# Late softmax division, scores in three split products, and experts with stationary weights

## The reference, cut to what matters

```
# layer 1: q from the rows, k and v from context and rows (120 + 256 = 376 keys)
sim = einsum('bhid,bhjd->bhij', q * 64**-0.5, k)
attn = softmax(sim, axis=-1)
out = einsum('bhij,bhjd->bhid', attn, v)
x = x + tanh(g_xattn[0]) * layernorm(out @ w_out)
...
# layer 4: g, u and the hidden layer of four experts, weighted by cw
g = einsum('th,ehi->tei', x, Wg); u = einsum('th,ehi->tei', x, Wu)
mlp_out = einsum('tei,eih->teh', silu(g) * u, Wd)
routed = einsum('te,teh->th', cw[:, :4], mlp_out)
# plus x times other columns of cw, plus a causal convolution of 4 taps
```

## Time and profile before

| | |
|---|---|
| runs (three) | 2227.55 us median, 2222.08 to 2231.18 |
| profiled execution | span 2225.1 us, mean granted TensorE clock 0.994 |
| busy over the span | PE 2186.7 us (98%), DVE 1728.1 (78%), ACT 1282.0 (58%), POOL 645.1 (29%) |
| first stage | about 0 to 1113 us, then the experts to about 1600 us |
| last stage | about 1600 us to the end |

### The profile page before, as it was taken

How to read it: one execution, slowest core, us unless ns; L and a number is a source line. 1 busy time by engine, 2 the same in 40 slices (tenths; PEclk the granted TensorE clock), 3 DMA queues, 4 the chain that set the end, 5 groups by cost and what they waited for, 6 DMA issues and landing times. The chain is left out here.

```text
span 2225.1 us, 48355 instructions
## 1 busy us (share of the span) xinstructions
PE 2186.7 (98%) x15486; PEld 1865.5 (84%) x15486; DVE 1728.1 (78%) x6112; ACT 1282.0 (58%) x3251; POOL 645.1 (29%) x1162
## 2 busy tenths in 40 slices
PE   8999999999999999999999999999999999999997
PEld 6777777777777777777699999999878888888886
DVE  6788888888888888888675555555579999999986
ACT  6776776776776776776443333433345555555553
POOL 1123223222232232232220000000355555555541
PEclk9999999999999999999899999999999999999999
DMA  5320110110110110110052222221212222222210
GB/s 189 124 97 22 37 40 23 37 39 21 40 38 20 39 39 20 40 32 27 11 161 73 81 86 72 81 77 41 89 58 65 65 65 64 65 65 65 65 39 20
DMA packets 111642, 129.57 MB, mean 58 GB/s; under 512 B 14898, under 2 KB 98089, under 8 KB 111264
## 3 DMA queue, kind: packets, MB, share of 16 engines
q1 hardware_dynamic: 98249, 105.06, 14.9%
q0 software_dynamic: 12288, 21.21, 3.3%
q10 hardware_dynamic: 855, 0.19, 0.0%
HBM read 84.26 MB, written 54.53 MB: 62 GB/s over the span
## 5 line engine op out<-in xcount | busy, mean ns | idle before, releaser
L711 ACT ACTIVATE a_prob<-a_prob,a_nmax 128x376 f32<-128x376 f32 x512 | 309.7, 606 | 155.3 <-DVE a_nmax L857 155.3
L1457 ACT ACTIVATE e_hidden<-e_first,keep_b 128x256 f32<-128x256 f32 x320 | 134.1, 471 | 283.3 <-PE e_first L80 282.8
L857 DVE CUSTOM_DVE_ANT_0 a_prob<-a_score,a_mask_row 128x376 f32<-128x376 f32 x512 | 266.6, 540 | 10.8 <-issue 5.6
L80 PE MATMUL e_second<-e_w,e_hidden 128*128 128x256 f32 x1920 | 239.5, 284 | 0.0
L80 PEld LDWEIGHTS e_second<-e_w,e_hidden 128*128 128x128 f32 x1920 | 232.6, 192 | 0.0
L869 DVE TENSOR_SCALAR a_prob<-a_prob,a_rden 128x376 f32<-128x376 f32 x512 | 220.9, 453 | 2.5
L1151 PE MATMUL a_turned<-keep_ident,a_prob 128*128 128x128 f32 (+1 forms) x1536 | 217.3, 277 | 2.8 <-DVE a_probT L876 1.6
L1151 PEld LDWEIGHTS a_turned<-keep_ident,a_prob 128*128 128x128 f32 (+1 forms) x1536 | 173.5, 142 | 43.5 <-issue 27.6
L1142 PE MATMUL a_score<-a_kT,a_qT 64*128 64x376 f32 x1024 | 196.4, 502 | 0.0
L876 DVE COPY a_probT<-a_turned 128x384 f32<-128x384 f32 x256 | 139.8, 546 | 54.4 <-PE a_turned L1151 54.4
L719 ACT ACTIVATE a_probT<-a_turned 128x384 f32<-128x384 f32 x256 | 124.9, 488 | 92.1 <-PE a_turned L1151 91.7
(11 more groups left out here) (237 smaller groups left out, 5231.1 us busy)
## 6 DMA issues: line engine op xcount, KB each, us to landing
w_in<-W SPq DMA_DIRECT2D x32, 512.0 KB, 4.1
slots<-a_zeros SPq DMA_DIRECT2D x8, 1280.0 KB, 8.7
keep_rows<-slots SPq DMA_DIRECT2D x40, 256.0 KB, 3.9
answers<-e_y SPq DMA_DIRECT2D x40, 256.0 KB, 2.2
a_xn<-x SPq DMA_DIRECT2D x32, 256.0 KB, 2.9
a_xr<-x SPq DMA_DIRECT2D x32, 256.0 KB, 3.8
x<-r_x SPq DMA_DIRECT2D x32, 256.0 KB, 4.0
w_in<-x SPq DMA_DIRECT2D x32, 256.0 KB, 2.6
```

Of the source, the lines that this page charges most:

```text
L80: last = nc.tensor.matmul(out, stationary(a, t), moving(b, t), start=start and n == 0, stop=stop and n == len(todo) - 1)
L711: nc.scalar.activation(prob[:, u % 4, a], prob[:, u % 4, a], ACT.Exp, bias=nmax[:, u % 4, a:a + 1], scale=-1.0, accum_out=den[:, u % 4, a: ...
L857: nc.vector.tensor_tensor_reduce(prob[:, u % 4, a], score[SCORE_AT[u][a]][:, 0:NKV], mask_row[:, p], -1.0, 3.0e38, ALU.add, ALU.min, nmax[ ...
L1457: nc.scalar.activation(hidden[:, 2 * j + i], first[:, j, i * CH:(i + 1) * CH], ACT.Relu, bias=b1[:, 2 * j + i, bass.ds(e, 1)]).then_inc(re ...
```

## The change

**First stage.** Scores are a split product: q and k get a low part (`q_low`, `k_low` on DVE), and `scores` issues the three passes, the two heads in turn. The division moves behind `times_v`: `normalise` goes, `turn_prob` takes the bare exponentials, and `attended` on DVE multiplies the result (128x256 per pair of heads) by the reciprocal sums. There these lie along the free axis and are equal on 64 partitions. To get them there, `over_sum` (now once per pair of heads) takes the reciprocal and transposes it in 32x32 blocks, and `spread_shares` on SP writes it to DRAM in four transfers, waits, and reads it back in two that copy it to 64 partitions each. A bank that `q_high` or `k_high` reads is free only after `q_low` or `k_low`. `place`, `choose` and `counts_in` change their places, the router's count moves on PE, and POOL sends a batch's rows in one piece.

**Last stage.** In `gate_up` the weights become stationary and the 256 rows stream: half of the experts (`j`) at a time, 12 matmuls of 256 columns where there were 6 of 512. The hidden layer is then born transposed, `turn_hid` goes, and the router's weight must lie along the free axis: `weights_turned` (DVE), `spread_weights` (SP: four writes, a wait, one read to 128 partitions, 512 KB) bring it there. `share_ups` and `hidden` (DVE, 128x512 each, twice a step) take the place of `weigh`. `silu(1)`, `hidden_low(0)`, `down`, `x3_own` and others change places; `x4p` gets a second buffer.

```diff
+            def spread_shares(b, m):
+                done = KI * b + m
+                eng.wait_ge(rden_ok, done + 1)
+                for g in range(0, P, 32):
+                    eng.dma_start(t["shares"][m, :, g:g + 32], rden_rows[g:g + 2 * QT, m % 2]).then_inc(share_out, 16)
+                eng.wait_ge(share_out, 64 * (done + 1))
+                at_least(eng, att_ok, done - KI + 1)
+                for a in range(2):
+                    eng.dma_start(share[64 * a:64 * a + 64, m], ...).then_inc(share_in[m], 16)
...
+            def k_low(b, m):
+                eng.wait_ge(k_hi, KI * b + m + 1)
+                nc.vector.tensor_tensor(kT[:, 1, m], (bank_b if m < 2 else bank_a)[:, 0:NKV], kT[:, 0, m].bitcast(F32),
+                                        ALU.subtract).then_inc(k_lo, 1)
+            def q_low(b, i):
+                eng.wait_ge(q_hi, 2 * b + 2 - i)
+                nc.vector.scalar_tensor_tensor(qT[:, 1, 2 * i:2 * i + 2], bank_a[:].rearrange("p (m s) -> p m s", m=2),
...
-            def normalise(b, u, a):
-                nc.vector.tensor_scalar(prob[:, u % 4, a], prob[:, u % 4, a], rden[:, u % 4, a:a + 1], None, ALU.mult) \
...
+            def attended(b, m):
+                eng.wait_ge(pv_made, KI * b + m + 1)
+                eng.wait_ge(share_in[m], 32 * (b + 1))
+                nc.vector.tensor_tensor(att[:, m], (bank_a if m == 1 else bank_b)[:, 0:S], share[:, m],
+                                        ALU.mult).then_inc(att_ok, 1)
...
-                    nc.tensor.matmul(score[SCORE_AT[u][a]][:, 0:NKV], qT[rows, p, m, i * P:(i + 1) * P],
-                                     kT[rows, p, m], start=True, stop=True).then_inc(score_ok[a], 1)
+                for n, (high, low) in enumerate(PASSES):
+                    for a in range(2):
+                        rows = slice(64 * a, 64 * a + 64)
+                        last = nc.tensor.matmul(score[SCORE_AT[u][a]][:, 0:NKV], qT[rows, high, m, i * P:(i + 1) * P],
+                                                kT[rows, low, m], start=n == 0, stop=n == len(PASSES) - 1)
...
+            def spread_weights(b):
+                eng.wait_ge(cw_turned, b + 1)
+                for g in range(0, P, 32):
+                    eng.dma_start(t["chosen"][:, g:g + 32], cw_rows[g:g + EM * QT]).then_inc(cw_out, 16)
+                eng.wait_ge(cw_out, 16 * 4 * (b + 1))
+                at_least(eng, share_ok[1], b)
+                eng.dma_start(cw_wide[:].rearrange("p e s -> p (e s)"),
+                              t["chosen"].rearrange("c q -> (c q)").partition_broadcast(P)).then_inc(cw_in, 16)
...
-                for e in range(EM):
-                    es = slice(e * P, (e + 1) * P)
-                    nc.vector.scalar_tensor_tensor(hid[:, i, es], hs[:, i, es], cw[:, p, i, e:e + 1], ups[i][:, es],
+            def share_ups(b, j):
+                eng.wait_ge(cw_in, 16 * (b + 1))
+                nc.vector.tensor_tensor(hid[:, j].rearrange("p (e s) -> p e s", e=2),
+                                        ups[j][:].rearrange("p (e s) -> p e s", e=2), cw_wide[:, pair(j)],
+            def hidden(b, j):
+                nc.vector.tensor_tensor(hid[:, j], hs[:, j], hid[:, j], ALU.mult).then_inc(hid_ok[j], 1)
...
-                split_product(nc, out[i][:].rearrange("p (e i) -> p e i", e=EM),
-                              lambda a, k: x4T[:, a, k, i * P:(i + 1) * P],
+                for e in range(2):
+                    last = split_product(nc, out[j][:, e * S:(e + 1) * S], lambda a, k: weight2(name, a, k)[:, 2 * j + e],
+                                         lambda a, k: x4T[:, a, k], KD)
```

More of the change, by code:

```diff
@@ L928, in step @@
                     weights_lower(3, wo[:], stage_o)
-                if live(s - 2):
-                    normalise(s - 2, 2, 0)
                 if live(s - 3):
-                    att_low(s - 3, 3)
+                    attended(s - 3, 3)
                 if live(s - 2):
@@ L979, in step @@
                     row_max(s - 2, p, 6, 0)
+                if here(s - 4):
+                    choose(eng, s - 4, 4)
+                if live(s - 2):
                     row_max(s - 2, p, 6, 1)
-                    over_sum(s - 2, 4)
-                    normalise(s - 2, 4, 0)
-                    normalise(s - 2, 4, 1)
+                    over_sum(s - 2, 2)
+                if here(s - 4):
+                    choose(eng, s - 4, 5)
+                if live(s - 2):
+                    turned_out(s - 2, 3, 1)
+                    attended(s - 2, 0)
+                if here(s - 4):
+                    choose(eng, s - 4, 6)
+                if live(s - 2):
+                    row_max(s - 2, p, 7, 0)
+                if here(s - 4):
+                    choose(eng, s - 4, 7)
+                if live(s - 2):
+                    row_max(s - 2, p, 7, 1)
+                if live(s - 1):
+                    q_low(s - 1, 1)
+                if live(s - 2):
                     att_low(s - 2, 0)
-                    turned_out(s - 2, 3, 1)
-                    row_max(s - 2, p, 7, 0)
-                    row_max(s - 2, p, 7, 1)
+                if live(s - 1):
+                    k_low(s - 1, 0)
                 if here(s - 3):
@@ L2337, in step @@
                 if live(s - 4):
-                    weigh(s - 4, p, 1)
+                    hidden(s - 4, 0)
+                    relu(s - 4, p)
+                    share_ups(s - 4, 1)
+                    hidden(s - 4, 1)
                 if live(s - 3):
                     silu(s - 3, 0)
+                if live(s - 4):
+                    hidden_low(s - 4, 0)
+                if live(s - 3):
                     route_and_combine(s - 3, q, s, p)
@@ L2366, in down @@
                         eng.wait_ge(wd_low, 1)
[L2367 to L2368 removed]
+                for i in range(QT):
+                    for n, (a, c, e) in enumerate((a, c, 2 * j + e) for e in range(2) for a, c in PASSES):
+                        last = nc.tensor.matmul(total[:, i * D:(i + 1) * D], hid2[:, a, e, i * P:(i + 1) * P],
+                                                wd2[:, c, e], start=j == 0 and i == 0 and n == 0, stop=False,
+                                                skip_group_check=True)
+                last.then_inc(down_made[j], 1)
             def values(b):
```

425 lines of the change are left out of this document (215 added, 210 removed).

## The result

The changed kernel takes 2332.26 us (median of 4 runs, 2329.41 to 2334.39), the one before 2228.14 in the runs beside it: 1.047 times as long, with an interval of 1.0447 to 1.0493. I had forecast slower, but 2276 and at most 2320. The profiled execution has a span of 2329.3 us, 104.2 more than before.

The account below looks back on a forecast made before the run. The prediction took a ring through several engines to bound each changed stage. To 2225.1 us it added 31 (first stage), 13 (last stage) and 6 (ends), 2275.1, and said 2276, with a range of 2190 to 2320.

Parts of the forecast that it names:

- rings: First and last stage: closed paths through several engines, adding up to the step, 33.58 and 18.48 us.
- The chain keeps its length: Last stage, router's chain on DVE up to cws: stays at 5.42 us.
- The middle leg: Last stage, normalise4 to the chain's first operation, 9.14 us: grows by 0.69.
- the first leg: Last stage: cws to normalise4, -0.28 us. Where the choice is discussed: first stage, out_stat to row_max, +1.24.
- the right ring: First stage, path from out_stat through DVE, ACT and TensorE back to out_stat: +1.0 us a step, bounds 0.2 to 1.8.
- By legs: First stage: out_stat to row_max +1.24 us, row_max to router_in's end -0.37, turn_prob to output +0.62.
- the choice: First stage, DVE between out_stat and row_max: about ten tiny operations of choose come in, 0.89 us.
- TensorE's work: TensorE alone would allow steps of 32.9 us in the first stage, 17.4 to 17.8 in the last.
- The round trips: Transfers to DRAM and back, division about 7 us, weights 7.8: covered in the steady state, costed at nothing.
- That the rings might be looser: First rival, both stages: TensorE sets both steps, 2189 us, range 2175 to 2216; chance 0.20.
- The fourth rival: First stage scores: two heads don't overlap in the fast format, blocks of 2.2 us, +90, 2334 in all; chance 0.07.
- the third rival: Last stage: the weights' round trip comes late, 1.4 us a step, +43, 2320 in all; chance 0.12.

Follow-up runs that it names:

- The first experiment: Changed kernel with the last stage's POOL addition (x3p + x4r) cut to two columns per partition: 2301.79 us.
- experiments 4 and 5: Changed kernel without q_low and k_low; the former with three score products of high parts, 2273.83 us, the latter with one full-float32 product, 2289.09 us.
- experiment 4: Changed kernel without q_low and k_low, the scores' three products reading the high parts: 2273.83 us.
- experiment 2: Changed kernel without both round trips through DRAM and the waits for them, reciprocal sums and router's weights constant: 2329.42 us.

## Why the prediction was wrong

**The direction and its reason were right.** Both stages were rings, TensorE's smaller work bought nothing, and both steps grew. What failed first was a term of the last stage, which had been put at nothing.

**The step that failed: "The chain keeps its length".** It grew from 5.42 to 6.48, by 1.06 us in the step shown. I had read what each DVE operation costs and put it on DVE's own queue, but I had not asked what runs on POOL at the same time. The change moves `x3_own` to the end of ACT's step and the addition behind `norm3` on POOL, so the addition starts when the chain has begun. The first experiment shows its price: 1.08 by the median step, and 29 us in all.

**The middle leg was mis-sized.** +0.69 was forecast, +1.16 measured. The four new operations took 2.63 instead of 2.40 (1895.92 to 1896.52, 1897.43 to 1898.03, and 1898.56 to 1899.99 with a gap of 0.19 in it), and `own_heads` waits 0.24 for TensorE. This is 0.47 a step, 15 us. The four operations are inside their bound of 4 x 0.68 = 2.72, but the bounds had no term for that wait: with the first leg, -0.28 forecast and -0.21 measured, the two legs come to +0.95, above the +0.73 that I gave as the most.

**First stage: the right ring for a part of the way.** +1.0 was forecast for the step, +1.43 measured, within the bounds of 0.2 to 1.8. By legs the working looks better than it was, and that is luck: +1.24 against +1.37, -0.37 against -0.38, +0.62 against +0.67. Its sum was +1.09, rounded down to 1.0. What I left out is 0.13 before `out_stat`; and the slack before `times_v` shrank by 0.32 and not 0.40. But 0.89 of the first leg was the choice, and moving it away changed nothing. Nor did DVE run without a gap there before, as I had said: it waits 0.27 for ACT at 713.40, which I took out as a term further on. The ring there is the one through `project_q` and `q_high`, and what lengthened it lies behind `q_low`: from the end of the first `q_high` to `row_max` it was 720.46 - 715.28 = 5.18 us before and is 715.35 - 708.50 = 6.85 now. That q and k's low parts are what costs was right (experiments 4 and 5). ACT's `q_high`, before and after:

```profile
714.68 0.60 ACT L697 ACTIVATE a_qT<-keep_bank 128x512 f32<-128x512 f32 x1 [0.94 <-PE keep_bank L80]
```
```profile
707.90 0.60 ACT L718 ACTIVATE a_qT<-keep_bank 128x512 fp32r<-128x512 f32 x1
```

**TensorE's work was right in the first stage, and too small in the last, without effect.** 32.9 was forecast and is what TensorE is busy in a step of experiment 4. Two errors cancel in it. A score block of 12 matmuls takes 1.21 to 1.23 (713.42 to 714.63 on TensorE), less than my 1.30, so four blocks save 1.0 and not 0.66; some 0.3 has come in elsewhere, in `output` among others (2.96 instead of 2.83 to its successor), and I didn't follow it all. In the last stage 17.4 to 17.8 was forecast, while TensorE is busy 18.14 of the step.

**The round trips** were costed at nothing in the steady state, and no cost of them can be measured (experiment 2). The transfer's 4.1 us came out as taken from the earlier trace rows, and not as the estimate of 3.2 that stood beside it. The +6 for the ends can't be told apart: all that lies outside the two stages' steps is +4.2.

**The rivals.** That the rings might be looser had 0.20; the choice had such slack, but both steps grew, and so the rival falls. The fourth rival's time of 2334 is within 2 us of the measured 2332, and that is chance: its mechanism, two heads that don't overlap in the fast format, needed blocks of 2.2, and they are 1.22. The upper end of 2320 was the third rival's. What happened, a meeting of two engines, was in none of them, and so no range had a term for it.

## What the runs showed of the hardware

While a POOL addition of two SBUF operands ran (1.3 us), DVE operations with two inputs in SBUF were held up and ended 0.03 to 0.55 us after it: the blend (0.47 to 1.53), `hidden` (0.68 to 1.27), `hidden_low` (0.68 to 1.52), the last tap (1.68 us lost), and `f_sel` (0.16 to 1.26). Operations beside it with one of their inputs in PSUM, as the pieces of `weigh` (1.11 for four), were not. In the first stage of the changed kernel `att_low`, otherwise 0.42, is held by POOL's addition for `r_xb`:

```profile
717.58 0.97 DVE L926 TENSOR_TENSOR a_att<-a_att 128x256 fp32r<-128x256 f32 x1 [0.40 <-ACT a_att L747]
```
```profile
716.96 1.31 POOL L638 TENSOR_TENSOR r_xb<-a_xr,a_bo 128x512 f32<-128x512 f32 x1
```

One SBUF input can be enough. In the kernel before, two `normalise` on end, 128x376 with one large input, which is in SBUF, take 0.73 to 0.77 elsewhere in the step, but 1.35 to 1.71 in each of the 12 steps between 500 and 900 us where POOL's addition for `r_xb` runs. In the step below the first of the two takes 1.08 instead of 0.40 and ends 0.2 after POOL:

```profile
726.05 1.40 DVE L869 TENSOR_SCALAR a_prob<-a_prob,a_rden 128x376 f32<-128x376 f32 x2
```
```profile
725.61 1.29 POOL L615 TENSOR_TENSOR r_xb<-a_xr,a_bo 128x512 f32<-128x512 f32 x1
```

It goes the other way as well. POOL's `o_var` takes 0.19 elsewhere; here it starts 0.03 behind `hidden` and ends 0.06 after it. And in experiment 2 the addition starts with the first blend at 1858.76: the blend takes its 0.47, the addition 1.62 instead of 1.29, and the second blend, which comes later, is the one held (1.36). The rows of `o_var` and `hidden`:

```profile
1897.46 0.71 POOL L1752 TENSOR_SCALAR o_var<-o_mv 128x2 f32<-128x2 f32 x1
```
```profile
1897.43 0.68 DVE L2205 TENSOR_TENSOR f_hid<-f_hs,f_hid 128x512 f32<-128x512 f32 x1
```

The Trainium skill says in "SBUF — State Buffer", Who interferes with whom, that a DVE instruction with two SBUF inputs contends with a GpSimd instruction that reads SBUF, and that the shared port pair is an exclusive lock, where the order of issue decides who is blocked. The trace agrees in what is held up, by the blend's 1.06 and `o_var`'s 0.52 behind an operation that had begun before. In one row the order is less plain: the taps begin at 1888.24, the last of the four at 1889.42 and would be over at 1889.9, and the addition is shown to start at 1890.00. Either POOL's start in the record is late, or the port was held before it; no run tells.

## What to carry to other kernels

When a change moves an operation on GpSimd, or puts new operations with SBUF inputs on VectorE, draw both queues side by side: a GpSimd operation of 1.3 us cost VectorE 0.6 to 1.7 us here, and moving it helps only if it lands beside operations that read PSUM or off the path that sets the step.

An engine without gaps isn't proof that its work is on the ring: another path can be just as long. Moving one piece away tests it in one run; here 0.9 us of work left a leg and nothing was gained. The same holds for a chain of rows that adds up to the period: it shows one path of that length, not that there is no other.

A cheaper product is worth what the bound allows. Here the 0.8 us a step that TensorE saved on scores was bought with six subtractions on the engine that fed it, and they cost the step 35.03 - 33.29 = 1.74.
